# First convolution of a graph network: the centring of the gathered rows on ScalarE, one instruction per tile

## The chip, the cores and the metric

One core of one Trainium2 chip. The core has TensorE (PE in the profile, its weight loads PEld), VectorE (DVE), ScalarE (ACT), GpSimd (POOL), SyncE (SP) and 16 DMA engines. The metric is the device time of one execution in microseconds (us); lower is better.

## What is computed

The input is 50,000 nodes of 64 numbers and 25,000 edges (`src`, `dst`, sorted by `dst`). Each layer normalises the nodes and then passes messages along edges. The changed place is in the first spline convolution, whose input is the normalised node row:

```python
def _layernorm(x, axis=-1, eps=1e-05):
    m = jnp.mean(x, axis=axis, keepdims=True)
    v = jnp.var(x, axis=axis, keepdims=True)
    return (x - m) / jnp.sqrt(v + eps)
...
    xk = jnp.einsum('ni,kio->nko', x, W)             # 25 kernel matrices
    ...  msg = sum over 4 corners of basis * xk[src, idx]
    agg = jax.ops.segment_max(msg, dst, num_segments=N)
    agg = jnp.where(jnp.isfinite(agg), agg, jnp.zeros_like(agg))
    return agg + x @ root + bias
...
h = jnp.maximum(_layernorm(x, axis=-1), 0.0)
x = x + conv2(relu(conv1(h)))
h = jnp.maximum(_layernorm(x, axis=-1), 0.0)
x = x + attention_over_edges(h)
```

The kernel doesn't form `xk` for all nodes. It gathers the row `x[src]` of every edge, centres and normalises it there (a second time, beside the normalisation of all nodes), multiplies it with the hat weights of the edge and with the 25 matrices.

## The kernel before

The edges are cut into 49 groups of 4 tiles of 128 edges; the nodes into 49 groups of 1024 rows (128 partitions of 8). The first convolution runs group by group, edges and nodes side by side, in the span from about 150 to 700 us. There is no planner: every engine has a `step(g)` written out by hand, run by `each`, which unrolls 3 groups, then loops over 4 groups at a time for 40 groups, and then unrolls the rest. What ties engines together are counting semaphores (`wait(engine, steps, group, name)`); `norm` counts mean, eps and rstd of a group, `ecen` and `ncen` the centring of edge rows and node rows, `esq` and `nsq` their squares, `z` the four spread tiles, `zt` their transposes, `prod` the four products.

In one step of group g:

- POOL issues 4 indirect gathers (L584, of group g+3, which need the gather buffer free, that is `ecen` of g+1) and 4 indirect scatters (L591, of group g-1, which need the row that ACT writes at L807, and the row numbers of L765 and L767).
- DVE runs, in this order: `node_in` (L1360), `scaled` (L1283), `weigh` 0 (L1332, which waits for PE's product), `sums` of group e = g+2 (L1397 for the edges, L1401 for the nodes), spread tile 0 (L1312), `mean` of e (L1411, which writes the negative means), spread tile 1 (L1312), `centre_rows` of e (L1417 edges, L1422 nodes), `weigh` 1, the scan (L1324), `variances` (L1429, L1432), spread tile 2, eps (L1439), `weigh` 2, spread tile 3, `weigh` 3, the reciprocal (L1449), the adds (L1340, L1346, L1353) and `node_out` (L1378).
- ACT runs: the index copies (L673, L765, L767), the evacuation of transposed tile pair 2 (L755), the square of the centred edge rows (L782), the square of the centred node rows (L787), the relu of the turned nodes (L790), the evacuation of tile pair 3 (L755), the square root (L798), evacuations 0 and 1 of the next group (L755, twice), and the row for the scatter (L807).
- PE runs: the products of tile pair 0 (L964), turns of tiles 2 and 3 (L957), of the messages (L984), of the nodes (L995), turn of the next tile 0, the products of tile pair 1 (L964, of which the second part waits for evacuation 3 on ACT), the turn of the next tile 1, the root products (L1006) and the turn back (L1032).

Of the kernel before, what the change touches and what calls it, by code (L numbers as in the profile page):

```python
# [27 lines left out]
ALU = mybir.AluOpType  # L28
ACT = mybir.ActivationFunctionType
AX = mybir.AxisListType.X  # L30

P = 128
C = 64
K = 5
TPG = 4
# [68 lines left out]
def wait(eng, steps, g, name=None):  # L104

    value = steps.at(g, name)
    if not isinstance(value, int) or value > 0:
        eng.wait_ge(steps.sem, value)
# [9 lines left out]
def build(nc, a, out):  # L118
# [5 lines left out]
    G = EGROUPS  # L124
# [11 lines left out]
    with ExitStack() as ctx:  # L136
        def sb(name, shape, dt=F32):
            return ctx.enter_context(nc.sbuf_tensor(name, shape, dt))
# [29 lines left out]
        bias = [sb(f"bias{i}r", [P, C]) for i in (1, 2)]  # L168
# [69 lines left out]
        gath = [sb(f"gath{i}", [P, TPG, 2, ROW]) for i in range(SLOTS)]  # L238
# [3 lines left out]
        lnc = sb("lnc", [P, 2 * TPG, C])  # L242
        lnq = sb("lnq", [P, 2 * TPG, C])
        a0r = sb("a0r", [P, TPG, KR])
        jst = sb("jst", [P, 5, TPG + NPP])
# [98 lines left out]
        def half_of(g):  # L344

            return slice(g.parity * TPG, g.parity * TPG + TPG)
# [310 lines left out]
        def _(act):  # L657
# [88 lines left out]
            def conv(n):  # L746
                s = cs[n]

                def step(g):
# [12 lines left out]
                    if n == 1 and (g - 1).within(G):  # L762
                        e = g - 1
# [13 lines left out]
                        act.activation(back_tiles_of(idxI, g), gath[g.slot(SLOTS)][:, :, 0, C], ACT.Copy)\  # L777
                            .then_inc(s["idx"].sem, 1)
                    if n == 1 and (g + 2).within(G):
                        wait(act, s["ecen"], g + 2)  # L780
                        wait(act, s["evar"], g + 1)
                        act.activation(lnq[:, 0:TPG, :], lnc[:, half_of(g), :], ACT.Square)\  # L782
                            .then_inc(s["esq"].sem, 1)
# [18 lines left out]
                    if (g - 1).within(G):  # L802
                        e = g - 1
                        wait(act, s["at"], e)
                        if n == 2:
# [3 lines left out]
                            .then_inc(s["row"].sem, 1)  # L809

                each(act, step, 3, 1, ahead=3)

            act.wait_ge(s_w, WEIGHTS)
# [313 lines left out]
        def _(dve):  # L1127
            V_ = nc.vector
# [146 lines left out]
            def conv(n):  # L1275
                s = cs[n]
                jsum, jmean, jv, jy, jt = (jst[:, k, :] for k in range(5))
# [134 lines left out]

                def centre_rows(g):
                    wait(dve, s["norm"], g, "mean")
                    if g.within(G):
                        wait(dve, s["z"], g - 2, "z3")
                        V_.tensor_tensor(lnc[:, half_of(g), :], gath[g.parity][:, :, 0, 0:C],  # L1417
                                         jmean[:, 0:TPG].unsqueeze(2).broadcast_to([P, TPG, C]), ALU.add)\
                            .then_inc(s["ecen"].sem, 1)
                    if (g - 1).within(G):  # L1420
                        wait(dve, s["xn"], g - 2)
                        V_.tensor_tensor(nln[:, :, :], nx[1 - g.parity][:, :, 0:C],  # L1422
                                         jmean[:, TPG:].unsqueeze(2).broadcast_to([P, NPP, C]), ALU.add)\
                            .then_inc(s["ncen"].sem, 1)
# [16 lines left out]
                def step(g):  # L1441
# [25 lines left out]
                    if stats:  # L1467
                        centre_rows(e)
# [172 lines left out]
```

## Time and profile before

| | |
|---|---|
| median of 3 runs | 1922.77 us (1921.35 to 1923.86) |
| the profiled execution | 1922.7 us |
| its span in the trace | 1920.9 us |
| first convolution, from first to last L1417 | 150.5 to 666.3 us, 49 groups |

The span is what the trace shows from the first to the last instruction; 1.8 us of the profiled execution lie around it. The profile says for each engine how long it was busy, for each group of instructions how long one takes, and what ended the idle time in front of it. In the timeline each line is one or more instructions: start, length, engine, line, written tile, read tiles, and in brackets the idle time in front with its releaser. Instructions of one engine overlap: the start of the next one can lie before the end of the last.

### The profile page before, as it was taken

How to read it: one execution, taken by the hardware profiler on the slowest of the kernel's cores; microseconds unless marked ns; L12 is line 12 of the kernel's file. 1: busy time of each engine (PE TensorE's matmuls, PEld its weight loads, DVE VectorE, ACT ScalarE, POOL GpSimd, SP SyncE). 2: the span in 40 equal slices, each digit the busy share in tenths (PEclk: the TensorE clock that was granted, in tenths of full speed). 3: DMA queues.
4: the chain of work that ended last, by engine and by line, in shares of the span. 5: the costliest groups of instructions: out<-in, count | busy, mean ns of one | idle time of the engine just before them, and what ended most of it. 6: DMA issues, size and time to landing. Idle time of an engine off the chain costs nothing.

```text
span 1920.9 us, 33986 instructions
## 1 busy us (share of the span) xinstructions
PE 1583.3 (82%) x7745; PEld 1024.9 (53%) x7745; DVE 1560.4 (81%) x2878; ACT 697.3 (36%) x1743; POOL 1209.6 (63%) x1207
## 2 busy tenths in 40 slices
PE   1987898989899869999999999977777777777774
PEld 1254566656666656777777777754433334334342
DVE  2588899999999958899889899867777777777775
ACT  1463333333333332333323223235333444444432
POOL 4004777777777757777767767514666666666664
PEclk9998999999999989999999999989888888888887
DMA  8942444444444436877777777732323222323220
GB/s 136 164 55 61 96 106 104 103 102 103 106 103 105 95 100 181 233 225 229 232 218 232 230 220 226 225 84 57 64 63 63 63 63 63 64 62 63 63 57 12
DMA packets 408085, 232.10 MB, mean 121 GB/s; under 512 B 305989, under 2 KB 381958, under 8 KB 408046
## 3 DMA queue, kind: packets, MB, share of 16 engines
q1 hardware_dynamic: 312158, 152.47, 29.8%
q0 software_dynamic: 44864, 65.52, 15.3%
q10 hardware_dynamic: 51024, 13.68, 5.6%
q8 instruction: 14, 0.23, 0.0%
q14 instruction: 25, 0.20, 0.0%
HBM read 141.71 MB, written 92.64 MB: 122 GB/s over the span
## 4 chain that ended last, share of the span: by engine, by line
PE 39%; issue 9%; ACT 7%; DVE 7%; POOL 1%; DMA 1%; DVEq 0%; ACTq 0%; SPq 0%; POOLq 0%
PE bank L964 16%; PE bank L1085 5%; PE bank L1104 3%; PE bank L957 3%; PE bank L1006 2%; PE bank L1023 2%; DVE arena L1554 2%; ACT arena L869 2%; PE bank L995 1%; ACT lnq L876 1%; DVE arena L1542 1%; ACT arena L866 1%; PE bank L1015 1%; PE bank L984 1%; PE bank L1032 1%
## 5 line engine op out<-in xcount | busy, mean ns | idle before, releaser
L964 PE MATMUL bank<-Wk,arena 128*128 128x320 f32 (+1 forms) x2352 | 655.6, 464 | 56.7 <-ACT arena L755 56.7
L964 PEld LDWEIGHTS bank<-Wk,arena 128*128 128x128 f32 (+1 forms) x2352 | 327.3, 189 | 303.1 <-issue 221.7
L584 POOL DMA_INDIRECT gath<-T,gidx x392 | 385.8, 984 | 149.3 <-issue 113.0
L584 POOL DMA_INDIRECT gath<-M,gidx x196 | 196.2, 1001 | 206.3 <-ACT gidx L828 107.9
L584 POOL DMA_INDIRECT gath<-in_x_dram,gidx x196 | 197.5, 1008 | 189.3 <-ACT gidx L673 130.8
L755 ACT ACTIVATE arena<-bank 128x256 f32<-128x256 f32 (+1 forms) x392 | 169.3, 432 | 308.2 <-PE bank L957 307.6
L591 POOL DMA_INDIRECT T<-srow,sidx x196 | 216.1, 1103 | 80.4 <-issue 58.7
L591 POOL DMA_INDIRECT out_dram<-srow,sidx x196 | 198.3, 1012 | 75.7 <-issue 59.7
L1332 DVE TENSOR_TENSOR arena<-bank,A 128x320 f32<-128x320 f32 x392 | 191.5, 489 | 66.1 <-PE bank L964 58.7
L957 PE MATMUL bank<-ident,arena 128*128 128x128 f32 x980 | 171.6, 274 | 13.1 <-DVE arena L1312 13.1
L1085 PE MATMUL bank<-arena,Wqk 128*128 128x512 f32 x98 | 79.1, 900 | 117.8 <-DVE arena L1542 117.8
L957 PEld LDWEIGHTS bank<-ident,arena 128*128 128x128 f32 x980 | 124.4, 142 | 44.1 <-issue 7.3
L1584 DVE RECIPROCAL arena<-bank 128x256 f32<-128x256 f32 x49 | 86.1, 1758 | 73.5 <-PE bank L1119 73.5
L860 ACT ACTIVATE arena<-bank 128x512 f32<-128x512 f32 x49 | 29.3, 597 | 276.9 <-PE bank L1095 276.9
L1324 DVE TENSOR_TENSOR_SCAN arena<-ends_cut,arena,bank 64x512 f32<-64x512 bf16 x98 | 123.9, 1264 | 0.3 <-PE bank L984 0.3
L1078 PE MATMUL bank<-DT,spread 128*128 (+1 forms) x392 | 118.1, 431 | 0.0
L1006 PE MATMUL bank<-rootpair,nhT 128*128 128x128 f32 x784 | 103.6, 275 | 0.0
L1078 PEld LDWEIGHTS bank<-DT,spread 128*128 128x128 f32 x392 | 84.4, 228 | 31.9 <-issue 23.4
L1006 PEld LDWEIGHTS bank<-rootpair,nhT 128*128 128x128 f32 x784 | 95.4, 192 | 0.3
L1312 DVE TENSOR_TENSOR arena<-lnc,a0r 128x320 f32<-128x320 f32 x196 | 93.7, 480 | 0.0
L1104 PE MATMUL bank<-lnq,means 128*128 128x512 f32 x98 | 53.7, 630 | 42.7 <-ACT lnq L876 42.7
L1085 PEld LDWEIGHTS bank<-arena,Wqk 128*128 128x128 f32 x98 | 19.7, 251 | 129.3 <-DVE arena L1542 129.3
(185 smaller groups left out, 2800.8 us busy)
## 6 DMA issues: line engine op xcount, KB each, us to landing
arena<-T SPq DMA_DIRECT2D x48, 816.0 KB
T<-arena SPq DMA_DIRECT2D x96, 272.0 KB
T<-zero ACTq DMA_DIRECT2D x1, 13281.2 KB, 103.8
B<-arena SPq DMA_DIRECT2D x49, 256.0 KB
arena<-B SPq DMA_DIRECT2D x49, 256.0 KB, 3.6
arena<-in_x_dram SPq DMA_DIRECT2D x48, 256.0 KB, 4.1
out_dram<-arena SPq DMA_DIRECT2D x48, 256.0 KB
begins_cut<-begins_d SPq DMA_DIRECT2D x49, 128.5 KB, 3.4
```

The source lines that it names most:

```text
L584: pool.indirect_dma_start(out=gath[slot][:, j, k, 0:width], out_offset=None, in_=table, in_offset=bass.IndirectOffsetOnAxis(gidx[slot][:, ...
L591: pool.indirect_dma_start(out=table, out_offset=bass.IndirectOffsetOnAxis(sidx[g.parity][:, j:j + 1], 0), in_=srow[g.parity][:, j, 0:width ...
L755: act.activation(ZT[j // 2][:, first:first + chunks, :], bank[j % 2][:, 0:chunks * P], ACT.Relu)\
L957: tr = pe.transpose(bank[j % 2][:, c * P:c * P + P], Z[g.parity][:, j // 2, (first + c) * P:(first + c + 1) * P], ident[:, :])
L964: return pe.matmul(bank[2 + r][:, 0:KO], ZT[q][rows, chunk, :], Wk[n - 1][rows, weights].rearrange("p k o -> p (k o)"), start=start, stop= ...
L1006: mm = pe.matmul(bank[7][:, q * P:q * P + P], nhT[:, q * P:q * P + P], root[n - 1][:, :], start=True, stop=True)
L1078: pe.matmul(bank[b + e.parity].rearrange("p (t h e) -> p h t e", h=2, e=P)[:, j], spread[:, j, :], pairs, start=(j == 0), stop=False, skip ...
L1085: pe.matmul(bank[b + g.parity][:, :], W[:, :, :].rearrange("p t c -> p (t c)"), XT[g.parity][:, :], start=False, stop=True, skip_group_che ...
L1104: pe.matmul(bank[7][:, :], means[:, :], squares, start=True, stop=True).then_inc(at["var"].sem, 1)
L1312: V_.tensor_tensor(Z[g.parity][:, j // 2, at_:at_ + KO].rearrange("p (k c) -> p k c", c=C), row.broadcast_to([P, K, C]), w.unsqueeze(2).br ...
L1324: V_.tensor_tensor_scan(agg[g.parity][:, ::-1], ends_cut[g.parity][:, ::-1], bank[4][0:C, ::-1], agg[1 - g.parity][:, 0:1], ALU.add, ALU.max)\
L1332: V_.tensor_tensor(V[:, j].rearrange("p (k o) -> p k o", o=C), bank[2 + j % 2][:, 0:KO].rearrange("p (k o) -> p k o", o=C), A1[:, bass.ds( ...
```

## The change

VectorE's centring of the gathered edge rows (one operation over 4 tiles of 64 numbers, 128x256) is taken out of `centre_rows`. ScalarE does it in its own step, right ahead of the square that reads it, with four activations of 128x64, each with its column of the negative means as the bias. The wait for the mean, the wait for the spread tiles that still read the buffer, and the signal `ecen` go along with it. The centring of the node rows stays on VectorE.

```diff
                     if n == 1 and (g + 2).within(G):
-                        wait(act, s["ecen"], g + 2)
+                        e = g + 2
+                        wait(act, s["norm"], e, "mean")
+                        wait(act, s["z"], g, "z3")
+                        for j in range(TPG):
+                            centred = act.activation(lnc[:, e.parity * TPG + j, :], gath[e.parity][:, j, 0, 0:C],
+                                                     ACT.Identity, bias=jst[:, 1, j:j + 1])
+                        centred.then_inc(s["ecen"].sem, 1)
+                        wait(act, s["ecen"], e)
                         wait(act, s["evar"], g + 1)
                         act.activation(lnq[:, 0:TPG, :], lnc[:, half_of(g), :], ACT.Square)\
                             .then_inc(s["esq"].sem, 1)
...
                 def centre_rows(g):
                     wait(dve, s["norm"], g, "mean")
-                    if g.within(G):
-                        wait(dve, s["z"], g - 2, "z3")
-                        V_.tensor_tensor(lnc[:, half_of(g), :], gath[g.parity][:, :, 0, 0:C],
-                                         jmean[:, 0:TPG].unsqueeze(2).broadcast_to([P, TPG, C]), ALU.add)\
-                            .then_inc(s["ecen"].sem, 1)
                     if (g - 1).within(G):
                         wait(dve, s["xn"], g - 2)
                         V_.tensor_tensor(nln[:, :, :], nx[1 - g.parity][:, :, 0:C],
```

On VectorE, in the loop body, from the mean to the scan. Before:

```order
L1411 TENSOR_SCALAR jst<-jst 128x12 [waits c1_ecen,c1_ncen,c1_nsum,c1_esum]
L1312 TENSOR_TENSOR arena<-lnc,a0r 128x320 [waits c1_turn,c1_a0r]
L108 REGISTER_ALU
L1417 TENSOR_TENSOR lnc<-gath,jst 128x256 [waits c1_z,c1_norm]
L1422 TENSOR_TENSOR arena<-arena,jst 128x512 [waits c1_xn]
```

The same place now (lines below the edit have moved by 7, and below the removed lines by 2: L1418 is the former L1411, L1319 the former L1312, L1424 the former L1422):

```order
L1418 TENSOR_SCALAR jst<-jst 128x12 [waits c1_ecen,c1_ncen,c1_nsum,c1_esum]
L1319 TENSOR_TENSOR arena<-lnc,a0r 128x320 [waits c1_turn,c1_a0r]
L108 REGISTER_ALU
L1424 TENSOR_TENSOR arena<-arena,jst 128x512 [waits c1_xn,c1_norm]
```

The centring of the edge rows is gone; the node rows follow directly on the spread tile.

On ScalarE, in the loop body, from evacuation 2 to evacuation 3 (L789 is the former L782, L794 the former L787, L797 the former L790):

```order
L755 ACTIVATE arena<-bank 128x256 [waits c1_turn]
L108 REGISTER_ALU
L108 REGISTER_ALU [waits c1_norm]
L784 ACTIVATE lnc<-gath,jst 128x64 [waits c1_z]
L784 ACTIVATE lnc<-gath,jst 128x64 x3
L108 REGISTER_ALU
L789 ACTIVATE lnq<-lnc 128x256 [waits c1_evar,c1_ecen]
L794 ACTIVATE arena<-arena 128x512 [waits c1_nvar,c1_ncen]
L108 REGISTER_ALU
L797 ACTIVATE nhT<-bank 128x512 [waits c1_npe]
L755 ACTIVATE arena<-bank 128x384 [waits c1_turn]
```

Four activations and a wait for the mean, which hangs on a register instruction, now stand between evacuation 2 and the square; the order of the others is as it was. PE, POOL and SP issue the same instructions as before.

## Rows read from the trace of the kernel before

**Rows 1.** The page: busy time, share of the span, instructions, by engine.

```profile
PE 1583.3 (82%) x7745; PEld 1024.9 (53%) x7745; DVE 1560.4 (81%) x2878; ACT 697.3 (36%) x1743; POOL 1209.6 (63%) x1207
```

**Rows 2.** Waits, 200 to 640 us: who waited for whom, total us, times, longest.

```profile
PE bank L964 <- ACT arena L755: 47.9, 41, 1.6
...
DVE arena L1332 <- PE bank L964: 12.6, 50, 0.3
```

**Rows 3.** Timeline of VectorE, 424 to 437 us, one group.

```profile
424.26 0.68 DVE L1360 TENSOR_TENSOR arena<-arena,jst 128x512 f32<-128x512 f32 x1
...
425.31 0.49 DVE L1332 TENSOR_TENSOR arena<-bank,A 128x320 f32<-128x320 f32 x1 [0.26 <-PE bank L964]
425.72 0.41 DVE L1397 TENSOR_REDUCE jst<-gath 128x4 f32<-128x256 f32 x1
...
427.04 0.16 DVE L1411 TENSOR_SCALAR jst<-jst 128x12 f32<-128x12 f32 x1
...
427.52 0.42 DVE L1417 TENSOR_TENSOR lnc<-gath,jst 128x256 f32<-128x256 f32 x1
427.85 0.68 DVE L1422 TENSOR_TENSOR arena<-arena,jst 128x512 f32<-128x512 f32 x1
...
436.54 0.41 DVE L1397 TENSOR_REDUCE jst<-gath 128x4 f32<-128x256 f32 x1
```

**Rows 4.** Timeline of ScalarE, 423 to 437 us.

```profile
426.61 0.38 ACT L755 ACTIVATE arena<-bank 128x256 f32<-128x256 f32 x1 [2.83 <-PE bank L957]
427.96 0.42 ACT L782 ACTIVATE lnq<-lnc 128x256 f32<-128x256 f32 x1 [0.97 <-DVE lnc L1417]
428.57 0.63 ACT L787 ACTIVATE arena<-arena 128x512 f32<-128x512 f32 x1 [0.18 <-DVE arena L1422]
429.10 0.58 ACT L790 ACTIVATE nhT<-bank 128x512 f32<-128x512 f32 x1
429.58 0.48 ACT L755 ACTIVATE arena<-bank 128x384 f32<-128x384 f32 x1
```

**Rows 5.** Timeline of TensorE in the same group.

```profile
430.19 2.08 PE L964 MATMUL bank<-Wk,arena 64*128 64x320 f32 x8 [1.12 <-ACT arena L755]
```

**Rows 6.** Timelines, 412 to 420 us: a loop turn's first group, where the wait hangs on a register.

```profile
416.62 0.42 DVE L1417 TENSOR_TENSOR lnc<-gath,jst 128x256 f32<-128x256 f32 x1
...
417.14 0.42 ACT L782 ACTIVATE lnq<-lnc 128x256 f32<-128x256 f32 x1 [1.07 <-DVE lnc L1417]
...
419.37 1.81 PE L964 MATMUL bank<-Wk,arena 64*128 64x320 f32 x7 [1.22 <-ACT arena L755]
```

**Rows 7.** ScalarE with a pointer as bias and without; timeline, and two lines' instructions.

```profile
44.91 4.21 ACT L685 ACTIVATE A<-vcol,knots 128x196 f32<-128x196 f32 x10
...
L881 ACT ACTIVATE arena<-bank,eps_col x49: 687/687/688, 1313.5 to 1896.2; 128x512 f32<-128x512 f32 x49
...
L772 ACT ACTIVATE arena<-bank x49: 597/597/599, 729.4 to 1264.3; 128x512 f32<-128x512 f32 x49
```

**Rows 8.** POOL: timeline from 424 us, then its groups of instructions, 200 to 640 us.

```profile
424.45 1.40 POOL L591 DMA_INDIRECT T<-srow,sidx  x1 [0.32 <-issue]
426.15 1.00 POOL L591 DMA_INDIRECT T<-srow,sidx  x1 [0.30 <-issue]
...
L591 POOL DMA_INDIRECT T<-srow,sidx x160 | 176.0, 1100 | 50.8 <-issue 48.9 <-ACT srow L767 1.8
L584 POOL DMA_INDIRECT gath<-in_x_dram,gidx x163 | 163.6, 1003 | 49.7 <-issue 49.7
```

**Rows 9.** Timelines of POOL and VectorE, 184 to 190 us: a scatter that takes longer.

```profile
185.64 1.84 POOL L591 DMA_INDIRECT T<-srow,sidx  x1 [0.30 <-issue]
...
185.94 0.68 DVE L1422 TENSOR_TENSOR arena<-arena,jst 128x512 f32<-128x512 f32 x1
```

**Rows 10.** Start of the first convolution, timelines of VectorE and ScalarE, 148 to 155 us.

```profile
150.30 0.17 DVE L1411 TENSOR_SCALAR jst<-jst 128x12 f32<-128x12 f32 x1
...
151.03 0.42 ACT L782 ACTIVATE lnq<-lnc 128x256 f32<-128x256 f32 x1 [1.48 <-DVE lnc L1417]
```

## The prediction

> **What bounds the kernel now.** I read the page first. VectorE is busy 81% of the span and ScalarE 36% [rows 1], which makes a move of work from the one to the other look like a plain gain. That share is no bound by itself, so the second view is the waits of the first convolution between 200 and 640 us, a stretch of 41 groups. There TensorE waits for ScalarE once in each group, 47.9 us in all, 1.17 us a time, and VectorE waits for TensorE about once a group, 12.6 us over 50 times [rows 2]. An engine that waits for another in nearly every group doesn't set the pace alone.
>
> The third view is the timeline of one group, and in it I look for a ring: who waits for whom, all the way round. A group takes 436.54 - 425.72 = 10.82 us, measured at L1397 [rows 3]. From its wait for TensorE's product (0.26 us ahead of L1332 at 425.31) VectorE runs without a gap to the mean (L1411 ends at 427.20) and on through L1417 (ends at 427.94) and L1422 (ends at 428.53) [rows 3]. ScalarE's square L782 starts at 427.96, 0.02 us after L1417; L787 at 428.57, 0.04 us after L1422; then L790 and L755 follow back to back and L755 ends at 430.06 [rows 4]. TensorE has stood still for 1.12 us and goes on at 430.19 [rows 5]; from there it works through without a wait to the product that L1332 of the next group waits for. So the ring is: VectorE up to L1422, then ScalarE's L787, L790, L755, then TensorE, then VectorE again. A second look confirms it. In the first group of each loop turn, the square L782 waits through a register instruction and starts 0.10 us after L1417 ends (417.14 against 417.04) instead of 0.02, and TensorE's wait for L755 grows from 1.12 to 1.22 us [rows 5, 6]. A tenth lost on ScalarE in this place is lost by TensorE.
>
> There is a second pace-maker just below the first. POOL issues four scatters of 1.10 us and four gathers of 1.00 us a group, with 0.30 us between any two [rows 8]: 4 x 1.10 + 4 x 1.00 + 8 x 0.30 = 10.8 us. It has no idle time besides these gaps. So POOL could follow a shorter ring by some hundredths at most, as long as its instructions take what they take now.
>
> **What the removal is worth.** L1417 goes: L1422 starts 427.85 - 427.52 = 0.33 us earlier [rows 3]. If VectorE alone set the pace, 49 x 0.33 = 16 us would go. But what the ring needs from VectorE is only that L1422 ends in time for L787. It now ends at 428.20 on this group's clock, and it no longer decides: what L787 waits for is ScalarE itself, which has more to do.
>
> **What the addition costs.** On the same clock: the mean ends at 427.20. The wait for it hangs on a register instruction in each of the four unrolled groups of the loop, so the first activation starts 0.10 us later [rows 6], at 427.30. ScalarE is free by then: its L755 ended at 426.99 [rows 4]. Four activations follow, each i after the one before, and the last takes d. The square waits for the last one (another 0.03 us, as now behind L1417), and L787 can start 0.32 us behind the square: it takes 0.42 us and consecutive activations overlap by 0.10 (L787 at 428.57 takes 0.63, L790 starts at 429.10) [rows 4]. So L787 starts at 427.30 + 3i + d + 0.35 = 427.65 + 3i + d. It starts at 428.57 now; the two are equal at **3i + d = 0.92 us**.
>
> The size of i and d isn't in the trace for 64 columns with a pointer as bias; I bound it. The slope is (0.63 - 0.42) / 256 = 0.82 ns a column [rows 4], so 64 columns without a pointer take 0.42 - 192 x 0.00082 = 0.26 us. A pointer adds 0.09 us: L881 with one takes 0.687, L772 over the same shape without takes 0.597 [rows 7]. That gives d = 0.35. For i, with the common overlap of 0.10 it is 0.25. The ten biased activations L685 take 4.21 us together at 0.60 each [rows 7], one every 0.40, an overlap of 0.20: by that i = 0.15. I take the middle, i = 0.20, since one row is of another kind of output (strided) and the other of another operand: 3i + d = 0.95, that is 0.03 us a group later than now. With i from 0.15 to 0.25 the sum is 0.80 to 1.10, from 0.12 us earlier to 0.18 us later. The outer ends are: no cost of the pointer at all, 3 x 0.15 + 0.26 = 0.71, 0.21 us earlier; and L685 taken as it stands less 132 columns, i = 0.29, d = 0.49, 1.36, 0.44 us later.
>
> The Trainium skill, page "ScalarE: Activation LUTs", section "What ACT_TABLE_LOAD costs", prices an activation with a pointer as bias at 280 ns + 0.833 ns a column with an overlap of about 93 ns between neighbours; d would be 0.33 and i 0.24, 3i + d = 1.05 and the group 0.13 us longer. Of the overlap the trace shows both, 0.10 at L787 and 0.20 at L685 [rows 4, 7], so I let the rows have the forecast.
>
> **The other engines.** The order of everything else is unchanged. VectorE gets 0.33 us of slack behind L1422. The variances that read the squares come only after a weighing and the scan; what is left of the slack it waits for TensorE. The slack is worth nothing, since TensorE's time is set by L755. POOL's gathers need `ecen` of a group two before; it comes 0.3 us later or earlier, some microseconds before the gather, and no one waits. The spread tiles need the centred rows a full group later. The identity function brings no extra table load, since the copies and squares around it run without one now. At the start there is no ring yet, but a chain: the mean ends at 150.47 and the square starts at 151.03, 0.56 us later [rows 10]. Four activations in a row need about 0.03 + 0.95 + 0.03 = 1.0 us, so the first group starts 0.45 us later; I count 0.6 us for the start in all.
>
> **Sum.** 46 groups in the ring x 0.03 = 1.4 us, start 0.6 us, no gain elsewhere: the profiled execution's 1922.7 us become 1924.7. The median of the runs before, 1922.77, is the same within 0.1; I forecast **1924 us**, rounding to the side of the lower i, which more instances bear out.
>
> **Rivals.**
> 1. ScalarE's chain gets clearly longer, slower than before. It decides from 3i + d = 1.00 on, if a pointer operand keeps the neighbours from overlapping more than 0.10 us. With i = 0.25: 0.18 x 46 + 0.6 = 8.9 us, 1932. With L685's spacing as it stands: 0.44 x 46 + 0.6 = 21 us, 1944. For it speaks L787 to L790 [rows 4], against it L685's overlap [rows 7]. The page named above says the same by its figures, 0.13 x 46 + 0.6, that is 1929.
> 2. The chain gets shorter, and POOL decides how much of it counts. With i = 0.15 the ring would be 0.12 us shorter, with the outer end 0.21. POOL has to follow, and it needs 10.8 us. A part of that is not its own: the first scatter takes 1.40 us where its neighbour takes 1.00 [rows 8], and it starts at 424.45, in the middle of VectorE's L1360 (424.26 to 424.94), an operation with two inputs in SBUF [rows 3]. A scatter that starts at 185.64, next to L1417 and L1422, takes 1.84 and ends 0.86 us after L1422 does [rows 9]; that is what a scatter looks like that gets going only when VectorE's operation is over. If VectorE leads POOL by a little more, L1360 ends sooner under the scatter, and POOL's period falls by about half of what the ring gains: 0.06 to 0.10 x 46 = 3 to 5 us, 1918 to 1920; without any hold by POOL 0.21 x 46 = 10 us, 1913. The Trainium skill, page "SBUF — State Buffer", section "SBUF: two separate sides", has this as an exclusive lock on a port pair that GpSimd shares with VectorE operations with two SBUF inputs; the two places above agree with it.
> 3. VectorE is the bound after all and the 16 us come, 1907. Against it stand its waits for TensorE and the tenth of rows 6 that goes through.
>
> **How the numbers follow.** About 0.2% (3.8 us) can be told from no change here. The ring within 0.08 us a group of today: 0.50, times from 1919 to 1927. Rival 1: 0.30, of which a third beyond 1932. Rival 2 beyond 0.2%: 0.16, mostly 1913 to 1919. Rival 3: 0.04. The range that leaves out a tenth on either side is 1915 to 1933; the forecast's own is 1919 to 1927. Faster 0.20, same 0.50, slower 0.30.
>
> **What would show it.** In the timeline of the changed kernel: the first L784 0.10 us behind L1418 (the mean), four of them in 0.95 us, L794 starting 2.88 us after the group's L1404, the former L1397 (2.85 now: 428.57 - 425.72), and TensorE's wait for L755 still there, 1.1 to 1.2 us. VectorE's idle time ahead of L1339 (the former L1332) grows by 0.33 us a group, the time that was taken off it. POOL keeps its 0.30 us gaps if the ring doesn't grow. The forecast is wrong if four L784 take under 0.85 or over 1.0 us, if TensorE no longer waits for L755, or if VectorE shows no more idle time than before.

## The result, and the profile after

The changed kernel takes **1930.51 us** (median of 5 runs, 1929.06 to 1933.23); the kernel before, run beside it, 1922.77 (1921.35 to 1924.35). The ratio is 1.0042 with a 95% interval of 1.0028 to 1.0057: the change makes the kernel 0.4% slower. The profiled execution took 1929.67 us with a span of 1927.9, 7.0 us more than the span before.

In the code of the kernel after, lines 781 to 1414 of the kernel before stand 7 further down, and those from 1420 on 2 further; L784 is new. The page's line of busy times (busy us, share of the span, instructions) is the one to put beside [rows 1]:

```profile
PE 1590.1 (82%) x7745; PEld 1029.0 (53%) x7745; DVE 1552.0 (81%) x2829; ACT 744.0 (39%) x1939; POOL 1211.7 (63%) x1207
```

VectorE lost 49 instructions that held it for 0.33 us each, 16 us, but only 8 us of busy time. Most of the difference is L1441 (the former L1439, the eps of 12 columns): it takes 0.31 us in three groups of four where it took 0.16, and VectorE's wait for TensorE behind it takes that up. ScalarE gained 196 instructions and 47 us. The waits from 200 to 640 us (who for whom, total us, times, longest), the view of [rows 2]:

```profile
PE bank L971 <- ACT arena L755: 52.4, 40, 1.7
...
DVE arena L1339 <- PE bank L971: 28.6, 90, 0.4
ACT lnc L784 <- DVE jst L1418: 13.2, 40, 0.4
POOL T L591 <- ACT srow L767: 10.0, 19, 0.8
```

TensorE still waits for L755, now 1.31 us a time instead of 1.17. VectorE's waits for TensorE show 16 us more than before, but this view leaves out waits under 0.15 us, and the kernel before has one of 0.12 in each group. By the busy time from 200 to 640 us, 421.0 us before and 408.7 now, VectorE was idle 31.3 us instead of 19.0, 0.31 us a group more. The time taken off VectorE came back as idle time.

One group, timeline of VectorE, to be read beside [rows 3] (start, us, engine, line, operation; in brackets the idle time before it and what ended it):

```profile
427.07 0.49 DVE L1339 TENSOR_TENSOR arena<-bank,A 128x320 f32<-128x320 f32 x1 [0.26 <-PE bank L971]
427.48 0.41 DVE L1404 TENSOR_REDUCE jst<-gath 128x4 f32<-128x256 f32 x1
...
428.80 0.17 DVE L1418 TENSOR_SCALAR jst<-jst 128x12 f32<-128x12 f32 x1
428.87 0.49 DVE L1319 TENSOR_TENSOR arena<-lnc,a0r 128x320 f32<-128x320 f32 x1
429.27 0.69 DVE L1424 TENSOR_TENSOR arena<-arena,jst 128x512 f32<-128x512 f32 x1
...
434.34 0.49 DVE L1339 TENSOR_TENSOR arena<-bank,A 128x320 f32<-128x320 f32 x1 [0.40 <-PE bank L971]
```

L1424 has moved up to right behind the spread tile, 0.34 us earlier on the group's clock, and nobody uses it: ScalarE gets to its result later than before. The same group on ScalarE and TensorE, beside [rows 4, 5]:

```profile
429.08 1.06 ACT L784 ACTIVATE lnc<-gath,jst 128x64 f32<-128x64 f32 x4 [0.32 <-DVE jst L1418]
430.17 0.42 ACT L789 ACTIVATE lnq<-lnc 128x256 f32<-128x256 f32 x1
430.50 0.61 ACT L794 ACTIVATE arena<-arena 128x512 f32<-128x512 f32 x1
431.02 0.58 ACT L797 ACTIVATE nhT<-bank 128x512 f32<-128x512 f32 x1
431.49 0.48 ACT L755 ACTIVATE arena<-bank 128x384 f32<-128x384 f32 x1
```

```profile
432.10 2.08 PE L971 MATMUL bank<-Wk,arena 64*128 64x320 f32 x8 [1.27 <-ACT arena L755]
```

The four centring instructions take 1.06 us together. The node squares L794 start 430.50 - 427.48 = 3.02 us after the sums L1404, 0.17 us later than in the kernel before (428.57 - 425.72 = 2.85, [rows 3, 4]). One L784 alone (instructions of the line: shortest, median, longest in ns):

```profile
L784 ACT ACTIVATE lnc<-gath,jst x196: 331/332/349, 150.3 to 671.5; 128x64 f32<-128x64 f32 x196
```

So d = 0.33 us, and 3i = 1.06 - 0.33 = 0.73, i = 0.24.

Where the 7 us are: between the first and the last sums of the first convolution 519.6 us instead of 514.6 (+5.0), and in the attention stage, whose code is the same, 585.7 instead of 583.3 between the first and last reciprocal (+2.4). Everything between these two stages together took 659.5 instead of 659.6, and the first sums start 0.2 us earlier. The sums and the reciprocals of the kernel after, lines with the first and last start:

```profile
L1404 DVE TENSOR_REDUCE jst<-gath x49: 405/409/421, 149.6 to 669.2; 128x4 f32<-128x256 f32 x49
```

```profile
L1586 DVE RECIPROCAL arena<-bank x49: 1757/1758/1759, 1328.7 to 1914.4; 128x256 f32<-128x256 f32 x49
```

From the seventh to the forty-seventh group, the steady part, a group took 10.998 us on average and 10.856 before: **+0.14 us a group**.

### The profile page after: what moved, and what is told of

The parts are those of the page before. It is cut to its first block, busy times and chain, and to the rows that moved or that the text cites. A ratio compares the mean times of both kernels' runs of the same rounds, so it can differ in the third digit from the quotient of the medians.

```text
span 1927.9 us, 34181 instructions
## 1 busy us (share of the span) xinstructions
PE 1590.1 (82%) x7745; PEld 1029.0 (53%) x7745; DVE 1552.0 (81%) x2829; ACT 744.0 (39%) x1939; POOL 1211.7 (63%) x1207
## 4 chain that ended last, share of the span: by engine, by line
PE 40%; issue 9%; ACT 8%; DVE 6%; DMA 1%; POOL 1%; DVEq 0%; ACTq 0%; SPq 0%; POOLq 0%
PE bank L971 16%; PE bank L1092 6%; PE bank L1111 3%; PE bank L964 3%; PE bank L1013 2%; PE bank L1030 2%; ACT arena L876 2%; ACT lnq L883 1%; DVE arena L1544 1%; PE bank L1002 1%; ACT arena L873 1%; DVE arena L1556 1%; PE bank L1102 1%; PE bank L1022 1%; PE bank L991 1%
## 5 line engine op out<-in xcount | busy, mean ns | idle before, releaser
L755 ACT ACTIVATE arena<-bank 128x256 f32<-128x256 f32 (+1 forms) x392 | 169.4, 433 | 324.5 <-PE bank L964 324.0
L867 ACT ACTIVATE arena<-bank 128x512 f32<-128x512 f32 x49 | 29.3, 597 | 281.8 <-PE bank L1102 281.8
L1319 DVE TENSOR_TENSOR arena<-lnc,a0r 128x320 f32<-128x320 f32 x196 | 94.0, 482 | 0.0
L772 ACT ACTIVATE arena<-bank 128x512 f32<-128x512 f32 x49 | 29.3, 598 | 155.0 <-PE bank L1022 155.0
```

Source lines behind the costliest of these rows:

```text
L755: act.activation(ZT[j // 2][:, first:first + chunks, :], bank[j % 2][:, 0:chunks * P], ACT.Relu)\
L1319: V_.tensor_tensor(Z[g.parity][:, j // 2, at_:at_ + KO].rearrange("p (k c) -> p k c", c=C), row.broadcast_to([P, K, C]), w.unsqueeze(2).br ...
```

## The experiments

Two theories were left standing by the profile after. **Ring:** what ScalarE loses ahead of L755, TensorE loses, and so the group. **POOL:** POOL's eight indirect DMAs with their gaps fill the whole group, 10.8 us, and what changed is how long they take; in the kernel after the first gather took 1.28 us in three groups of four where it took 1.13 before.

Eight runs were made on two other chips, on which the kernel before itself took 2429.7 and 2435.1 us. There all engines stood still together for some microseconds at a time, and a group of the first convolution took 14 to 17 us on average; what held them isn't shown. Their times answer a question about that situation and not about the result's, so of these eight runs only lengths of instructions and distances inside a group are used. They come first, in short; the four runs that settle the matter follow.

**a_nobias, a_nobias2: the four instructions without the pointer.**

```diff
                         for j in range(TPG):
                             centred = act.activation(lnc[:, e.parity * TPG + j, :], gath[e.parity][:, j, 0, 0:C],
-                                                     ACT.Identity, bias=jst[:, 1, j:j + 1])
+                                                     ACT.Copy)
```

> The changed kernel, with the four activations as plain copies without a pointer (they leave the centring of the edge rows out: the mean isn't subtracted). They should be 0.16 us apart and take 0.26, 0.75 us in all instead of the 1.06 measured, so the square of the node rows starts 2.71 us after the sums instead of 3.02 (2.85 before the change). Theory, ScalarE's time alone: 0.14 us a group under the kernel before, 6 us faster, 1916. With POOL as second pace-maker at about 10.8 us a group: 1920 to 1922. Rival (pointer or not makes no difference, the dearer part is the count of instructions or the wait): as the changed kernel, 1930.

> The changed kernel, with its four ScalarE instructions of a group as plain copies without the pointer to the mean (the edge rows aren't centred, so the normalization of them is left out in part); everything else stands. In a trace with late DMA landings four such copies took 0.69 us, against 1.06 us with the pointer. RING THEORY (the row's way over VectorE, ScalarE and TensorE sets the period, and the pointer's 0.09 us an instruction is what made the change slower): the rows of L794 start 0.37 us earlier than in the changed kernel and 0.20 us earlier than in the kernel before, the period of conv 1 falls from 10.97-11.05 us to about 10.7, and the time to about 1917 us, below the kernel before. POOL THEORY (POOL's eight indirect DMAs of a group, 8.4 us and eight gaps of 0.30, are back to back and set the period; the ring only decides where it is longer than they are): the period stops at POOL's, 10.8 us, and the time is that of the kernel before, 1922-1925 us, with POOL waiting for nothing but its 0.30 gaps. If neither: 1930 us as with the pointer, and then the length of the four isn't the cause.

In this kernel the edge rows aren't centred. Times 2476.66 and 2479.47 us: 3.0% (2.0 to 4.1) and 2.4% (1.1 to 3.8) above the kernel before on the same chips, against the forecasts of a gain and against what the same kernel shows further down. That is not explained. The four instructions took 0.69 us together in both, and the distance from the sums to the node squares was most often 2.65 us (median of 40 groups 2.72 and 2.76): the pointer is what makes the four long.

**b_two: two more pointer activations in the kernel before.**

```diff
                         act.activation(lnq[:, 0:TPG, :], lnc[:, half_of(g), :], ACT.Square)\
                             .then_inc(s["esq"].sem, 1)
+                        for j in (0, 1):
+                            act.activation(lnq[:, TPG + j, :], lnq[:, TPG + 2 + j, :], ACT.Identity,
+                                           bias=eps_col[:, :])
```

> The kernel before, with two more activations of 128x64 with a pointer as bias on ScalarE, right behind the square of the edge rows and ahead of the square of the node rows; they write scratch that nothing reads, and VectorE still centres. Theory (the length of ScalarE's run between VectorE's mean and evacuation 3 sets the group's time): the square starts 2.25 us after the group's sums, two activations come 0.33 and 0.24 us later, so the square of the node rows starts at 3.06 instead of 2.85. The group gets 0.21 us longer and the kernel 46 x 0.21 = 10 us slower, about 1932. Rival (the 0.15 us a group come from the moved signals or from the row gathers, not from ScalarE's time): no change, 1923.

2480.26 us, from which nothing follows. The two activations took 0.57 us together, and the node squares started 3.05 us after the sums, 0.20 later than in the kernel before.

**b_evac, b_evac2, a_evac: the last evacuation ahead of the squares.** a_evac is the same move in the changed kernel.

```diff
                     if g.within(G):
                         evacuate(g, 2)
...
+                    if n == 1 and g.within(G):
+                        evacuate(g, 3)
...
-                    if g.within(G):
+                    if n == 2 and g.within(G):
                         evacuate(g, 3)
```

> The kernel before, with one move: in the first convolution ScalarE evacuates tile 3 right behind evacuation 2, ahead of both squares and the relu, instead of behind them. TensorE turned that tile long before, so its wait of 1.12 us a group for L755 should go. Theory: the ring over ScalarE is open then, and the next bound shows. If that is VectorE (its waits of 0.26 and 0.18 us a group go, 10.4 us): 0.4 x 46 = 18 us faster, 1904. If it is POOL (eight DMA instructions, 10.8 us at today's 1.40 and 1.13 us for two of them): 0 to 3 us faster, 1920 to 1923, with POOL without idle time beyond its 0.30 us gaps. Rival to the ring as a whole: no change, and TensorE waits elsewhere.

> The kernel before with one move on ScalarE in conv 1: the last evacuation of a group's transposes (L755, j = 3) is queued right behind the one before it, ahead of the squares and the node rows, so TensorE no longer waits for it behind them (1.17 us in each group before). VectorE still centres. RING THEORY: the row comes up to 1 us earlier and the period falls, to about 10.0 us, the time to 1885-1900 us. POOL THEORY: the wait of TensorE for L755 goes, but POOL's eight DMAs still take 10.8 us a group: TensorE and VectorE wait somewhere else instead, and the time stays at 1920-1925 us.

> The changed kernel (ScalarE centres) with the same move of evacuation 3 ahead of the centring. Theory: the longer run of ScalarE is off TensorE's path, so the loss of the change goes. If VectorE is the next bound, its 0.33 us a group now count: 15 us under the kernel before with the move. If POOL is, both kernels with the move are the same within 2 us. Rival (the loss comes from the later signal of the centring or from the reads of the gathered rows by ScalarE): 7 us slower than the kernel before with the move.

2420.84, 2433.05 and 2438.69 us: 0.8% (0.3 to 1.4), 0.7% (0.1 to 1.2) and 1.3% (0.4 to 2.2) above the kernel before there, where a gain or no change was forecast for the first two. The same kernels come back below.

**b_pool, a_pool: an attempt to relieve POOL.**

```diff
                 for j in range(TPG):
+                    rows = slice(0, 32 if width == U and j > 1 else P)
                     pool.indirect_dma_start(
...
-                        out_offset=bass.IndirectOffsetOnAxis(sidx[g.parity][:, j:j + 1], 0),
-                        in_=srow[g.parity][:, j, 0:width], in_offset=None, bounds_check=bound, oob_is_err=False,
+                        out_offset=bass.IndirectOffsetOnAxis(sidx[g.parity][rows, j:j + 1], 0),
+                        in_=srow[g.parity][rows, j, 0:width], in_offset=None, bounds_check=bound, oob_is_err=False,
```

> The kernel before with less work on POOL in conv 1: the third and fourth scatter of each group cover 32 rows in place of 128 (the other 96 rows of these tiles aren't written: left out). If POOL's time for one goes with its rows, each takes a few tenths less than its 0.98-1.00 us and POOL has up to 1 us a group to spare. POOL THEORY: the period falls by what POOL is given, until the ring stops it: 1890-1915 us, and POOL then waits for the row at L591. RING THEORY: nothing moves, 1921-1925 us, and all that POOL is given turns into its wait for the row.

> The changed kernel with the same relief of POOL as in b_pool (the same rows left out). It tells what the ScalarE centring costs once POOL isn't in the way. RING THEORY: 1929-1933 us, and 7-8 us above b_pool. POOL THEORY: it falls too, below 1925 us; its distance from b_pool is then the ring's own difference, 0.15-0.17 us a group or 6-8 us, if both are at the ring by then; if the distance is under 2 us, the +0.15 us a group of the change came from POOL's longer gathers (1.28 us in place of 1.13) and not from the ring.

2490.14 and 2511.57 us, and no verdict on either theory. The kernel leaves 96 rows of the third and the fourth tile unwritten. The edit didn't do what it was made for, and that is its one use. The scatters of b_pool (L592 there), half of them with 32 rows and half with 128, and the four of one group, the last two with 32:

```profile
L592 POOL DMA_INDIRECT T<-srow,sidx x196: 873/1007/1755, 182.6 to 958.7; - x196
...
439.34 1.18 POOL L592 DMA_INDIRECT T<-srow,sidx  x1 [3.90 <-ACT srow L768]
440.83 1.01 POOL L592 DMA_INDIRECT T<-srow,sidx  x1 [0.30 <-issue]
442.14 0.88 POOL L592 DMA_INDIRECT T<-srow,sidx  x1 [0.30 <-issue]
443.32 0.87 POOL L592 DMA_INDIRECT T<-srow,sidx  x1 [0.30 <-issue]
```

The shortest scatter of 32 rows takes 0.87 us, the shortest of 128 in the same run 0.99. A quarter of the rows takes a tenth of a microsecond off, about 0.2 us a group and not the 1 us hoped for. A POOL that issues fewer indirect DMAs wasn't tried.

**a_nobias3: the same kernel as a_nobias on a chip like that of the result.** On it the kernel before took 1925.02 us.

> The same kernel as a_nobias (the changed kernel with its four ScalarE instructions as plain copies without the pointer, so that the edge rows aren't centred), looked at once more, for the distance from the sums to the node squares and the period of the groups. The four take 0.69 us and the node squares start 2.65 us after the sums, 0.37 us before the changed kernel's. Where no engine stands still for another reason: RING THEORY a period of about 10.7 us; POOL THEORY 10.8 us, with POOL back to back.

1914.6 us in the one execution that there is, span 1912.8: 15 us below the changed kernel and 8 below the kernel before, by the profiles, and 10 below the one execution of the kernel before beside it. It leaves out the centring of the edge rows, so it isn't a kernel one could use; it says what the pointer costs. Waits, 200 to 640 us:

```profile
PE bank L971 <- ACT arena L755: 39.9, 42, 1.4
...
DVE arena L1339 <- PE bank L971: 21.3, 83, 0.3
ACT lnc L784 <- DVE jst L1418: 14.1, 41, 0.5
POOL T L591 <- ACT srow L767: 2.0, 1, 2.0
```

Timelines of VectorE, ScalarE and TensorE in one group:

```profile
430.66 0.42 DVE L1404 TENSOR_REDUCE jst<-gath 128x4 f32<-128x256 f32 x1
...
432.27 0.69 ACT L784 ACTIVATE lnc<-gath 128x64 f32<-128x64 f32 x4 [0.38 <-DVE jst L1418]
433.00 0.42 ACT L789 ACTIVATE lnq<-lnc 128x256 f32<-128x256 f32 x1
...
433.32 0.61 ACT L794 ACTIVATE arena<-arena 128x512 f32<-128x512 f32 x1
...
434.92 2.08 PE L971 MATMUL bank<-Wk,arena 64*128 64x320 f32 x8 [0.96 <-ACT arena L755]
```

Without the pointer each instruction takes 0.24 us and the four 0.69, TensorE waits 0.95 us a time, and a group takes 10.64 us on average. That is 0.21 us less than before for node squares that start 0.20 us earlier (2.65 against 2.85). The POOL theory in its plain form, a floor at 10.8 us, is refuted: POOL followed. How it followed shows in its groups of instructions, 200 to 640 us (count, busy us, mean ns, idle before), beside [rows 8]:

```profile
L591 POOL DMA_INDIRECT T<-srow,sidx x164 | 178.8, 1090 | 51.7 <-issue 49.8 <-ACT srow L767 2.0
L584 POOL DMA_INDIRECT gath<-in_x_dram,gidx x166 | 159.6, 962 | 50.6 <-issue 50.6
```

Its gaps are still 0.30 us, and its gathers have shrunk from 1.003 to 0.962 us: the first of each four takes 0.99 where it took 1.13. POOL's instructions are elastic. By the same sum as in the prediction POOL now needs 4 x 1.09 + 4 x 0.96 + 8 x 0.30 = 10.6 us, so it is still back to back and had nothing left to give; which of the two leads is told by VectorE's sums, which need POOL's gathers. They start 0.41 us behind the weighing ahead of them in 26 of 40 groups, with no wait for a gather, and up to 0.14 later in the others. So the ring decided, by a narrow margin.

**b_two3: ScalarE made late in the kernel before, by the edit of b_two.**

> The kernel before with two more 128x64 ScalarE activations with a pointer in each group, on scratch, between the squares of the edge rows and those of the node rows; nothing is taken from VectorE. They put the node squares 3.05 us behind the sums (2.85 before, 3.02 changed). THEORY (what counts is how late ScalarE reaches L755, whichever engine centres): as much slower as the changed kernel or a little more, a period of 11.0-11.06 us and 1929-1933 us. RIVAL (the change's cost came from the row's own way, L1424 no longer behind the centring or the squares later): 1922-1925 us, as before. The attention stage, whose code is the same in all kernels, took 602.1 us before, 605.1 changed and 605.3 in a_nobias3: if it is 605 here and in b_evac3 too, its place in time or its clock decides and not the change.

1931.41 us (1927.59 to 1935.54) against 1921.63 for the kernel before beside it; ratio 1.0045, 1.0028 to 1.0061: the changed kernel's loss, got without the change. The whole times agree in part by luck: the stage grew by 10.3 us, of which 6.7 lie in the steady part and most of the rest in its first six groups, and the attention stage came out 4.3 us shorter. The period of the steady part is what counts. One wait, 200 to 640 us, and timelines in one group:

```profile
POOL T L591 <- ACT srow L767: 22.6, 30, 3.8
...
432.14 0.41 DVE L1400 TENSOR_REDUCE jst<-gath 128x4 f32<-128x256 f32 x1
...
434.38 0.42 ACT L782 ACTIVATE lnq<-lnc 128x256 f32<-128x256 f32 x1 [0.97 <-DVE lnc L1420]
434.70 0.57 ACT L785 ACTIVATE lnq<-lnq,eps_col 128x64 f32<-128x64 f32 x2
435.18 0.61 ACT L790 ACTIVATE arena<-arena 128x512 f32<-128x512 f32 x1
```

The node squares start 435.18 - 432.14 = 3.04 us after the sums, and a group takes 11.02 us. POOL isn't the bound here: it waits for the row number in three groups of four. The four kernels stand in a row:

| kernel | sums to node squares, us | a group, us | VectorE centres |
|---|---|---|---|
| a_nobias3 | 2.65 | 10.64 | no |
| before | 2.85 | 10.86 | yes |
| changed | 3.02 | 11.00 | no |
| b_two3 | 3.05 | 11.02 | yes |

(Medians of 40 starts, and mean distances of the sums from the seventh to the forty-seventh group.) From the first to the last row 0.40 us on ScalarE make 0.38 us of a group. Whether VectorE still does its centring makes no difference: the changed kernel and b_two3 lie on the same line, one with 0.33 us less on VectorE. Nor does the longer eps instruction of the changed kernel: it takes 0.19 us in b_two3. That is the ring theory, and it prices VectorE's freed time at zero.

**b_evac3 and a_evac3: TensorE's wait for L755 taken away, by the edit of b_evac.**

> The kernel of b_evac once more: VectorE centres as before, and in conv 1 the last evacuation of the transposes (L755, j = 3) is queued ahead of the squares and node rows on ScalarE. RING THEORY: TensorE's wait of 1.12-1.22 us for L755 goes, and VectorE, which sat idle for some 0.3 us a group in the kernel before, is the next to be late: the period falls from 10.86 to 10.3-10.6 us and the time to 1897-1912 us. POOL THEORY (already weak, since a_nobias3 ran at 10.64 us a group): 1920-1925 us.

> The changed kernel with the same move of the last evacuation. It tells where the change's ScalarE time costs. THEORY (the 0.17 us later node squares cost only because L755, for which TensorE waits, is queued behind them, and VectorE was given 0.33 us that nobody could use): with L755 ahead of them the ScalarE time is off the path, VectorE is the next bound and has 0.33 us less to do, so the centring on ScalarE is now worth its VectorE time: 5-15 us below b_evac3, 1885-1905 us. RIVAL (the pointer instructions delay more than L755: the squares, the sums of squares behind them on VectorE, the roots): above b_evac3 by 3 us or more.

b_evac3: 1917.88 us, ratio 0.9978 (0.9963 to 0.9994), the fastest whole kernel here, yet a miss: the forecast was 1897 to 1912. a_evac3: 1926.24 us, ratio 1.0020 (1.0002 to 1.0038), 8.4 us above b_evac3 where it should have been below; its rival had it 3 us or more above. The waits of b_evac3, 200 to 640 us (L966 is the product there, L1399 the sums):

```profile
PEld bank L966 <- DVE arena L1334: 32.5, 40, 1.0
...
DVE jst L1399 <- DMA gath<-in_x_dram,gidx: 18.7, 40, 1.0
```

The wait for L755 is gone from the list. In its place VectorE waits for a gather in each of the 40 groups. The groups of POOL's instructions in b_evac3:

```profile
L591 POOL DMA_INDIRECT T<-srow,sidx x161 | 174.0, 1081 | 49.1 <-issue 49.1
L584 POOL DMA_INDIRECT gath<-in_x_dram,gidx x163 | 168.6, 1034 | 49.7 <-issue 48.5 <-ACT srow L767 1.2
```

No gap of POOL's is longer than 0.35 us, and 4 x 1.081 + 4 x 1.034 + 8 x 0.30 = 10.86 us; a group took 10.89. Here POOL is the bound, at nearly the period that the ring had before. The gain of b_evac3 isn't in its steady part, where a group takes 0.03 us longer than before: its first five groups took 43.7 us instead of 47.7, without the 2.9 us that the sixth sums of the kernel before wait for a gather. In a_evac3 the same two rows read:

```profile
L591 POOL DMA_INDIRECT T<-srow,sidx x156 | 167.0, 1070 | 58.8 <-issue 46.0 <-ACT srow L767 12.7
L584 POOL DMA_INDIRECT gath<-in_x_dram,gidx x157 | 166.8, 1062 | 47.9 <-issue 43.6 <-ACT srow L767 3.0 <-ACT srow L816 1.2
```

Its gathers are 0.03 us longer still, 10.93 us for the eight, and a group took 11.24. The rest is a few long stalls, VectorE's wait for a gather and after it POOL's for the row number. The waits of a_evac3 (L1406 is the sums):

```profile
DVE jst L1406 <- DMA gath<-in_x_dram,gidx: 41.2, 33, 4.0
...
POOL T L591 <- ACT srow L767: 12.7, 5, 3.3
```

Six such waits of 3.3 to 4.0 us stand in the stage. TensorE stands still in each, and behind each its granted clock was at half (1.2 GHz) for 3.4 to 6.8 us, while in the kernel before and in the changed one it was full from 164 us to the last sums. The profiled execution of a_evac3 was its slowest, 1936.62 us, so it shows more of this than the median holds. What is shown: with L755 out of the way the next bound is POOL, not VectorE, so the centring on ScalarE still gains nothing. Not shown is why it loses 8 us there; the rival's way, a wait of VectorE for the later squares, is not among its waits, the longer gathers and the stalls are, and what sets them off isn't in the trace.

**The attention stage.** It runs the same code in all of these kernels. From the first to the last reciprocal it took 583.3 us before, 585.7 in the changed kernel, 585.8 in a_nobias3, 586.0 in b_evac3, 585.6 in a_evac3, but 579.0 in b_two3:

```profile
L1587 DVE RECIPROCAL arena<-bank x49: 1757/1758/1759, 1336.8 to 1915.8; 128x256 f32<-128x256 f32 x49
```

It ranges over 7 us without any change to it. The stretch between the reciprocals in the kernel before, the changed one and b_two3 (length; busy time of PE, PEld, DVE, ACT, POOL; granted clock, DMA share, GB/s):

```profile
1324.10:1907.40 583.30, 420.50 (x1320) 228.37 (x1320) 429.13 (x573) 232.61 (x475) 370.04 (x372) 0.85 0.27 59
...
1328.70:1914.40 585.70, 425.94 (x1320) 230.57 (x1320) 429.36 (x573) 232.44 (x475) 369.47 (x372) 0.84 0.27 59
...
1336.80:1915.80 579.00, 414.80 (x1320) 225.29 (x1320) 429.20 (x573) 232.73 (x475) 372.37 (x372) 0.86 0.27 59
```

TensorE's granted clock and its busy time go with the length, and VectorE's and ScalarE's busy times don't: 0.86 in the shortest, 0.85 before, and 0.84 in the four of 585.6 to 586.0 us. I take the 2.4 us of the result's two profiles as part of this spread; what sets the clock there stays open. The sum for the first convolution alone is +5.0 us.

## Why the prediction went wrong where it did

The range, 1915 to 1933, held the time; the forecast, 1924, missed by 6.5 us. Rival 1 came, with a chance of 0.30. That its 1932 lies so near the measured 1930.5 is in part luck: the ring gave 5 us, and 2.4 came from the attention stage, which no part of the prediction speaks of.

- **What bounds the kernel: right.** The ring over L755 set the pace. a_nobias3 and b_two3 moved ScalarE by 0.20 us in opposite directions and the group followed by 0.21 and 0.17 us.
- **What the removal is worth, nothing: right.** VectorE's idle time grew by (31.3 - 19.0) / 40 = 0.31 us a group for a forecast 0.33. That it comes so near is in part luck: the group got 0.14 us longer and VectorE's own instructions, L1441 above all, grew by about as much.
- **The condition, 3i + d = 0.92 us: right.** Measured 1.06, so the condition gives +0.14 us a group; the groups gave +0.14. The node squares themselves start 0.17 us later, but take 0.61 us instead of 0.63.
- **The size of 3i + d: the step that failed.** d was 0.33 for a forecast 0.35. i was 0.24 for a forecast 0.20: I took the middle between the overlap of 0.10 at L787 and that of 0.20 at L685 [rows 4, 7], and the first was the right row. L685 writes a strided output of 196 columns, L784 and L787 write theirs without a stride; why L685 overlaps more isn't shown. With i = 0.24 my own sum is (3 x 0.24 + 0.33 - 0.92) x 46 = 6 us. The Trainium skill, page "ScalarE: Activation LUTs", section "What ACT_TABLE_LOAD costs", gave 0.33 and 0.24 and 0.13 us a group; the trace agrees to 0.01 us. By its price of 186 ns + 0.833 ns a column without a pointer a copy of 64 columns takes 0.239 us; a_nobias3 shows 0.240.
- **The start, +0.6 us: wrong.** The sums started 0.2 us earlier, and the first five groups took 46.8 us instead of 47.7, by the starts of L1404 and L1397. One group of the kernel before holds a single wait of the sums for a gather, 2.9 us, where the changed kernel's longest is 0.6; a_nobias3 and b_two3 have it too, with 3.1 and 2.8 us, so it isn't the change's doing; what sets it isn't shown. The steady part's 0.142 x 40 = 5.7 us so come out as 5.0 for the stage.
- **POOL keeps its gaps: right in three groups of four.** In the fourth it waits 0.70 us for the row number.
- **Rival 2, that POOL holds back a gain: half right.** Its instructions do get shorter or longer with the ring's phase, but a ring shorter by 0.20 us was followed wholly, not by half. It is another gain, that of b_evac3, that POOL stopped.
- **Rival 3, VectorE as the bound: refuted** by the table above.

The first L784 started 429.08 - 428.97 = 0.11 us behind the mean, as forecast (0.10); four of them took 1.06 us, outside the 0.85 to 1.0 that I had named as the limits. By that sign the forecast was wrong, though its range held.

## What to carry to other kernels

Work moved off a busy engine gains only if that engine's end is waited for; follow the ring of waits once round, and price the added work on the engine where it lands, ahead of the one instruction that the others wait for. Four small ScalarE instructions with a pointer took 1.06 us here where one VectorE operation over the same 256 columns took 0.42, so splitting an operation by tile must buy a real wait. Before taking a wait away, look for the engine whose instructions stand back to back at nearly the same period: it takes over at once.

## What the runs showed of the hardware

- A ScalarE activation of 64 columns took 0.332 us with a pointer as bias and 0.240 without; neighbours overlapped by 0.09 in both kinds (0.73 / 3 = 0.24 apart with, 0.45 / 3 = 0.15 apart without).
- An indirect DMA costs POOL about 1.0 us, with 0.30 us between two, and hardly less for fewer rows: 0.87 us for 32 against 0.99 for 128 at the shortest (b_pool).
- POOL's indirect DMAs get longer beside some VectorE operations. For the six kernels on the result's kind of chip, between 200 and 640 us, POOL's DMAs can be sorted by whether a VectorE operation of two tensors without a bank among its inputs (both in SBUF) lay over their start or their last 0.25 us. Those with none took 0.96 to 1.03 us. All those of 1.13 us and more, up to 1.52, had one. It is a condition and not enough by itself: most of those that had one took no longer than 1.03 either, and the 0.25 us were chosen after looking. Two neighbours of b_evac3 with the VectorE rows over them:

```profile
419.12 0.67 DVE L1342 TENSOR_TENSOR arena<-arena 128x512 f32<-128x512 f32 x1
419.18 1.43 POOL L584 DMA_INDIRECT gath<-in_x_dram,gidx  x1 [0.30 <-issue]
...
420.62 0.68 DVE L1380 TENSOR_TENSOR arena<-bank,bias1r 128x512 f32<-128x512 f32 x1
420.91 0.94 POOL L584 DMA_INDIRECT gath<-in_x_dram,gidx  x1 [0.30 <-issue]
...
421.23 0.68 DVE L1362 TENSOR_TENSOR arena<-arena,jst 128x512 f32<-128x512 f32 x1
```

The gather that starts under L1342, two inputs in SBUF, takes 1.43 us; the next starts under L1380, one input in PSUM, and takes 0.94. It fits POOL's following the ring of a_nobias3, where the first gather of each four is 0.14 us shorter. It goes the other way as well: in the changed kernel the first gather and the small L1441 are both long in the same groups and end together, at 433.09 and 433.07 us here.

```profile
431.81 1.28 POOL L584 DMA_INDIRECT gath<-in_x_dram,gidx  x1 [0.30 <-issue]
...
432.76 0.31 DVE L1441 TENSOR_SCALAR jst<-jst 128x12 f32<-128x12 f32 x1
```

In the groups where that gather takes 0.99 us, L1441 takes 0.16. The Trainium skill, page "SBUF — State Buffer", section "SBUF: two separate sides", names a port pair that one of the two holds for its whole instruction. The trace agrees that such operations delay POOL, but not that the second always waits for the whole of the first: L1362 (two inputs in SBUF) starts at 421.23 under the gather that has run since 420.91, and neither is longer than usual, 0.68 and 0.94 us.
